# A fused attention and mixture-of-experts layer: maxima computed ten steps ahead instead of twelve, with weight loads, magnitudes and small steps placed at other ticks

## The reference, cut to what matters

```python
x = x + attn(layernorm(x))            # causal, softmax over keys
x = x + ffn(layernorm(x))

# attn
qkv = x @ W_qkv + b_qkv
scores = einsum('bhqd,bhkd->bhqk', q, k) * scale      # masked above the diagonal
out = (softmax(scores) @ v) @ W_out + b_out

# ffn: its own layernorm, a gate, then the two best of 8 experts
w, idx = top_k(softmax(xn @ gate_w), 2)
h = gelu(xn @ w1[e] + b1[e])
output = sum over the two of w * (h @ w2[e] + b2[e])  + residual
```

## Time and profile before

| | |
|---|---|
| median of 3 runs | 978.37 us (976.83 to 978.54) |
| the profiled execution, its own time | 980.76 us |
| its span | 979.0 us |
| mean granted TensorE clock | 0.902 |
| TensorE, VectorE, ScalarE, GpSimd busy | 89%, 74%, 60%, 47% |

### The profile page before, as it was taken

One profiled execution on the slowest core, in us unless ns is written; L12 is line 12 of the kernel. 1 busy time (PEld: TensorE's weight loads), 2 busy tenths in 40 slices (PEclk: granted clock), 3 DMA queues, 4 the chain that ended last, 5 costly groups with the idle time before them and its releaser, 6 DMA issues.

```text
span 979.0 us, 21326 instructions
## 1 busy us (share of the span) xinstructions
PE 867.6 (89%) x6870; PEld 564.8 (58%) x6870; DVE 724.6 (74%) x1658; ACT 586.0 (60%) x1079; POOL 462.0 (47%) x561
## 2 busy tenths in 40 slices
PE   4999977786876998888887899999999999999996
PEld 3655422231332424334342588889889989998874
DVE  6678886877657697898977488795776776666664
ACT  2776565554857687676958474564545554455453
POOL 2000032342525656558585656775476554545441
PEclk9999977775887758778897899999999999999999
DMA  9988667745747757566544742343323332233221
GB/s 211 298 278 255 203 183 206 188 119 161 215 133 211 198 153 210 139 204 168 168 123 126 237 105 60 61 92 54 51 40 57 52 57 48 46 50 48 44 45 17
DMA packets 146327, 130.09 MB, mean 133 GB/s; under 512 B 59344, under 2 KB 128848, under 8 KB 146096
## 3 DMA queue, kind: packets, MB, share of 16 engines
q1 hardware_dynamic: 115648, 87.51, 32.3%
q0 software_dynamic: 15680, 18.95, 12.1%
q10 hardware_dynamic: 14896, 22.28, 7.1%
HBM read 83.63 MB, written 44.80 MB: 131 GB/s over the span
## 4 chain that ended last, share of the span: by engine, by line
PE 45%; DMA 13%; DVE 12%; issue 10%; POOL 9%; SPq 6%; ACT 3%; POOLq 1%; ACTq 0%; DVEq 0%
PE banks L758 12%; PE banks L776 11%; PE banks L577 4%; POOL out L1693 3%; PE banks L680 3%; DMA weighed_values<-arena 3%; DMA arena<-qk_parts 3%; PE banks L636 3%; PE banks L567 2%; DMA arena<-in_L_ffn_w 2%; PE banks L692 2%; POOL slot_tokens L1640 2%; POOL arena L1669 2%; PE banks L608 2%; PE banks L621 2%
## 5 line engine op out<-in xcount | busy, mean ns | idle before, releaser
L980 ACT ACTIVATE arena<-banks,arena 128x256 f32<-128x256 f32 (+1 forms) x312 | 152.7, 542 | 175.7 <-issue 121.5
L758 PE MATMUL banks<-arena,weights 128*128 128x256 f16 (+1 forms) x1872 | 205.0, 266 | 4.5 <-DVE arena L1475 2.3
L776 PE MATMUL banks<-weights,arena 128*128 x1704 | 194.1, 273 | 0.6 <-DVE arena L1503 0.5
L758 PEld LDWEIGHTS banks<-arena,weights 128*128 x1872 | 174.4, 98 | 30.8 <-issue 7.3
L1693 POOL DMA_INDIRECT out<-arena x71 | 116.3, 1639 | 151.7 <-DVE arena L1514 114.3
L776 PEld LDWEIGHTS banks<-weights,arena 128*128 128x128 f16 x1704 | 165.6, 98 | 20.9 <-issue 1.8
L636 PE MATMUL banks<-arena 50*128 50x128 f16 (+3 forms) x512 | 129.2, 354 | 25.0 <-ACT arena L906 4.7
L608 PE MATMUL banks<-arena 48*128 48x128 f16 (+3 forms) x512 | 104.8, 352 | 44.0 <-DMA arena<-qk_parts 14.5
L1501 DVE TENSOR_SCALAR arena<-arena 128x512 f16<-128x512 f32 (+1 forms) x156 | 77.0, 493 | 62.9 <-ACT arena L980 61.5
L636 PEld LDWEIGHTS banks<-arena 50*128 50x128 f16 x512 | 38.9, 103 | 135.3 <-issue 55.0
L1503 DVE SCALAR_TENSOR_TENSOR arena<-arena 128x512 f16<-128x512 f32 (+1 forms) x156 | 110.1, 706 | 5.6
(11 more groups left out here) (190 smaller groups left out, 1309.3 us busy)
## 6 DMA issues: line engine op xcount, KB each, us to landing
weights<-in_L_ffn_w ACTq DMA_DIRECT2D x16, 1024.0 KB, 7.9
arena<-in_L_ffn_w SPq DMA_DIRECT2D x32, 512.0 KB
qk_parts<-weights SPq DMA_DIRECT2D x64, 128.0 KB
arena<-qk_parts SPq DMA_DIRECT2D x128, 64.0 KB, 3.2
weighed_values<-arena SPq DMA_DIRECT2D x32, 256.0 KB
token_rows<-arena SPq DMA_DIRECT2D x12, 512.0 KB, 4.4
arena<-qk_parts SPq DMA_DIRECT2D x128, 32.0 KB, 3.3
arena<-weighed_values SPq DMA_DIRECT2D x32, 128.0 KB
```

The costliest lines, as they stand in the source:

```text
L758: m = pe.matmul(bank[:, c * TILE:c * TILE + WIDTH[j]], w1[:, k, wp, f:f + P], xp[:, k, 0:WIDTH[j]], start=(i == 0), stop=(i == len(terms) ...
L776: m = pe.matmul(bank[:, c * D:(c + 1) * D], hp[:, f, c * P:(c + 1) * P], w2[:, f // (FC // 2), wp, f % (FC // 2), :], start=(f == 0 and i ...
L980: m = act.activation(h_32[r % 2][:, c, 0:WIDTH[j]], banks[:, 1 + c2, c * TILE:c * TILE + WIDTH[j]], ACT.Gelu, bias=b1_now[j % 2][:, 2 * c2 ...
```

## The change

`AHEAD` becomes 10: combo (u, i) computes slot i of unit u + 2, where it computed slot i + 2 of unit u + 2 (i up to 2) or slot i - 3 of unit u + 3. The projection computes ten slots instead of twelve, and starts them two steps of `project` later. The steps of the path of the maxima move with it. The last four magnitudes ahead of the attention (two matrices) are taken one by one in the first two units. The eight middle matrices are loaded in two halves each, 14 ticks apart. `invert`, `keep_inverse`, `move_inverse` and `divide` of the first eight units come 10 ticks later, `find_scales_2` 18 ticks later, and the first six weight splits 8 to 18 ticks later.

```diff
-        AHEAD = 2 * M_SLOTS + 2
+        AHEAD = 2 * M_SLOTS
...
-                at(base - 14, "top_split", u + 1)
-                at(base + 5, "top_turn", u + 1)
-                at(base + 10, "top_copy", u + 1)
-                at(base + 16, "top_in", u + 1)
+                at(base - 4, "top_split", u + 1)
+                at(base + 9, "top_turn", u + 1)
+                at(base + 14, "top_copy", u + 1)
+                at(base + 19, "top_in", u + 1)
...
-            at(after + (130 if late else 102), "invert", u)
-            at(after + (136 if late else 112), "keep_inverse", u)
-            at(after + (176 if late else 136 if u % NG else 158), "move_inverse", u)
+
+            room = 10 if u < 2 * NG else 0
+            at(after + (130 if late else 102 + room), "invert", u)
+            at(after + (136 if late else 112 + room), "keep_inverse", u)
+            at(after + (176 if late else 136 + room if u % NG else 158 + room), "move_inverse", u)
             if u % 2 == 1:
-                at(after + (216 if late else 156), "divide", divmod(u // 2, KC))
+                at(after + (216 if late else 156 + room), "divide", divmod(u // 2, KC))
         for i in range(len(matrices) - EARLY):
-            at(i * 36 + 30, "load_weights", i + EARLY)
-            at(i * 36 + 92, "magnitude", (i + EARLY, 0))
-            at(i * 36 + 110, "magnitude", (i + EARLY, 1))
+            at(i * 36 + 30, "load_weights", (i + EARLY, 0))
+            at(i * 36 + 44, "load_weights", (i + EARLY, 1))
+            at(i * 36 + 96, "magnitude", (i + EARLY, 0))
+            at(i * 36 + 114, "magnitude", (i + EARLY, 1))
+        for i in range(2):
+            for half in range(2):
+                at((8, 25, 44, 64)[2 * i + half], "magnitude", (EARLY - 2 + i, half))
...
-        at(8 * 36 + 114, "find_scales_2", 0)
-
-        split_ticks = [410 + 40 * i for i in range(LENT)]
+        at(8 * 36 + 132, "find_scales_2", 0)
+
+        split_ticks = [428 + 38 * i for i in range(LENT)]
...
-        OPEN = B - AHEAD // (2 * KC)
-        opening = [divmod(i, M_SLOTS) for i in range(AHEAD)]
+        OPEN = B + -AHEAD // (2 * KC)
+        opening = [None] * (2 * KC * (B - OPEN) - AHEAD) + [divmod(i, M_SLOTS) for i in range(AHEAD)]
...
-                    if b >= OPEN:
+                    if b >= OPEN and opening[2 * KC * (b - OPEN) + c]:
                         maxima(*opening[2 * KC * (b - OPEN) + c])
...
-            def load_weights(e_, m_):
+            def load_weights(e_, m_, halves=(0, 1)):
+                chunks = (KC, FC)[m_]
+                a, z = chunks * halves[0] // 2, chunks * (halves[-1] + 1) // 2
                 act.dma_start(
...
-                w.wait_ge(sem(f"w_in{m_}{e_}"), 16)
+                w.wait_ge(sem(f"w_in{m_}{e_}"), 16 if i < EARLY else 32)
...
-            magnitude(B - 2, (0, 1))
-            magnitude(B - 1, (0, 1))
             for stage, n in timetable:
```

More of the change, by code:

```diff
@@ L820, in load_x @@
                 act.dma_start(x_in[b % 4], x_rows(b)).then_inc(sem(f"x_in{b % 4}"), 16)
-            def load_weights(e_, m_):
+            def load_weights(e_, m_, halves=(0, 1)):
+                chunks = (KC, FC)[m_]
+                a, z = chunks * halves[0] // 2, chunks * (halves[-1] + 1) // 2
                 act.dma_start(
-                    w_sb[:, e_, m_ * EW // 2:(m_ + 1) * EW // 2].rearrange("p (c n) -> p c n", c=(KC, FC)[m_]),
-                    t[("L0_ffn_w1", "L0_ffn_w2")[m_]][e_].rearrange("(c p) n -> p c n", p=P)).then_inc(
+                    w_sb[:, e_, m_ * EW // 2:(m_ + 1) * EW // 2].rearrange("p (c n) -> p c n", c=chunks)[:, a:z, :],
+                    t[("L0_ffn_w1", "L0_ffn_w2")[m_]][e_].rearrange("(c p) n -> p c n", p=P)[:, a:z, :]).then_inc(
                     sem(f"w_in{m_}{e_}"), 16)
@@ L1038, in scalar @@
                         w.wait_ge(sem(f"v_store{half}"), 16 * (B // 2))
-                    load_weights(*matrices[n])
+                    load_weights(*matrices[n[0]], n[1:])
                 elif stage == "high_weights":
```

## The result

The changed kernel took 982.06 us (median of 7 runs, 981.06 to 988.52) beside 978.0 us for the kernel before: ratio 1.0053, interval 1.0031 to 1.0074. It is slower by 0.5%, where 1.6% faster was forecast, and lies outside the range. Run again in a later session it gave 1.0044 (1.0021 to 1.0068). The profiled execution took 984.82 us, its span is 983.0.

The account below looks back on a forecast made before the run. TensorE's waits in the attention, for stacks and VectorE, were taken as the bound. Projection -1, first ten units -14 and the others -1 sum to -16 us, giving 962.4 us; the range was 949 to 978.

Parts of the forecast that it names:

- Projection, -1: Before the attention: two slots fewer save 1.5 us, the transpose waits 0.5 for GpSimd's split; -1 us, bounds +1.2 and -2.2.
- First ten units, -14: Start of the attention: 124.1 us become 110, between VectorE's floor and the path of the maxima; bounds 105 and 118.
- the waits only move: Rival: VectorE stays at 78% in the first units and the removed waits return as others; 977 us, chance 0.07.
- The reciprocal comes 10 ticks later: First ten units: 2.6 us more room behind a sums' DMA that was 4.64 us late, so TensorE's 3.98 us wait goes.
- Queues: First units: changed order around `top_in`, GpSimd's split and masks, and TensorE's transpose costs nothing; uncovered, the third mask costs 1.2 us.
- `top_in` in the other units, "stays ahead": Behind the first eight units, on SyncE's queue: `top_in` still goes out before `keep_inverse`, so what it stands behind changes little.
- Halves, nothing: Middle matrices' loads: eight more issues, 3.1 us, hidden on ScalarE; the magnitude's lead of 14.1 us exceeds the longest landing.
- The scales later, a gain of the 2.51 and 5.04 us: First ten units: scales 18 ticks (4.7 us) later cover the 2.51 us DMA wait behind TensorE's 5.04 us wait.
- Magnitudes singly, -3.90: Attention's start: four magnitudes in a row take VectorE 4.59 us; taken singly, TensorE's 3.90 us wait goes.
- Units 10 to 31, -1: Rest of the attention: 5.5 us of stack waits and 1 of low clock go, split costs 4, two slots 1.5; bounds -7, +10.
- the clock comes back: Rival: the granted clock in units 10 to 31 rises from 0.81 to 0.9; 944 us, chance 0.15.
- the path of the maxima binds: Rival: through the attention, units pay the copy's 3.1 us delay; with seven such units 984 us, chance 0.11.

Follow-up runs that it names:

- e1: Kernel before with only the lead of the maxima cut to ten slots and its path (split, transpose, copy, `top_in`) moved: 1.0007 of the kernel before.
- e6: Changed kernel with `invert`, `keep_inverse`, `move_inverse` and `divide` of the first eight units back at their old ticks: 0.9968 of the kernel before.
- e10: Changed kernel with the sums' steps of the first eight units, `find_scales_2` and the first six weight splits at their old ticks: 0.9972 of the kernel before.
- e9: The changed kernel again as it is, in a later session as yardstick: 1.0044 of the kernel before.
- e14: Kernel before with only `invert`, `keep_inverse`, `move_inverse` and `divide` of the first eight units ten ticks later: 1.0060 of the kernel before.
- e15: Kernel before with only `invert` and `keep_inverse` of the first eight units ten ticks later: 1.0067 of the kernel before.
- e18: Kernel before with `invert` and `keep_inverse` ten ticks later, `move_inverse` and `divide` twenty, in the first eight units: 1.0002 of the kernel before.
- e11: Changed kernel with sums' steps, scales and splits at old ticks, and also the copy at tick 10 and `top_in` at 16: 0.9941 of the kernel before.
- e17: Kernel before with only the middle matrices loaded in halves, 14 ticks apart: 0.9966 of the kernel before.
- e8: Changed kernel with each middle matrix in one load of 1 MB in place of halves: 1.0110 of the kernel before.
- e7: Changed kernel with `find_scales_2` and the first six weight splits at their old ticks: 0.9991 of the kernel before.
- e13: Changed kernel with sums' steps, scales and splits at old ticks, and the four magnitudes again in a row ahead of the attention: 0.9967 of the kernel before.
- e12: Changed kernel with sums' steps, scales and splits at old ticks, and the old lead of twelve slots and old path: 0.9963 of the kernel before.

## Why the prediction was wrong

*The windows, and that TensorE after 552 passes everything on.* About right: the last scores of unit 31 come 5.7 us later (545.5 for 539.8), the profiled execution is 984.82 - 980.76 = 4.1 longer.

*Projection, -1.* Right: 120.7 to 119.0.

*First ten units, -14.* A size off: -6.3, at the bound that I had given (118 us). The waits named did go (stacks, three long VectorE waits). VectorE is busy 93.76 of 117.8 us, 80%, where 88% was forecast and 78% was the sign of "the waits only move". The path of the maxima was computed rightly (in unit 1 the copy ended 134.98 - 129.6 = 5.4 us after the unit's begin, 5.2 by the prediction) and costs little: with the new lead and path alone the ten units are 122.0 (e1). The landing of `top_in`, for which the sum took 5.0 and 3.5 us (the 3.5 with no row behind it), was 2.8 at most in unit 5. What kept them from 110 are single long holds, units 5 and 7 above all (16.0 and 15.6 us); with the ten ticks taken back they are 113.1 (e6), near the forecast, but only while the scales are late as well (119.0 in e10).

*"The reciprocal comes 10 ticks later", counted among the gains.* **This is the step that failed**, together with *Queues*, "these three cost nothing". Taken back, the ten ticks give 0.8% in the changed kernel, 7.4 us (e6 beside e9), and put alone on the kernel before they cost 0.6% (e14). The text weighed `keep_inverse` (tick 26 of a unit) against `top_in` (19) alone. It didn't see that `keep_inverse` also falls behind `move_o` (22), and `move_inverse` behind the next stack loads (44), though both of these can stand and wait on SyncE. In unit 5 `keep_inverse` so went out 4.8 us after its reciprocal and `top_in` 7.3 us after its copy, and in e6 0.7 and 1.3. That is shown for this unit. As a sum it is not: the first ten units carry 5.5 us of the 7.4 between e9 and e6, and SyncE's waits at `move_inverse` 2.5. On the kernel before, a hold of `move_inverse` is shown as the cause for e15, since with distance to `keep_inverse` the loss is gone (e18); e14, which has the changed kernel's own ticks, loses 0.6% without it. So which step failed is shown, and through which wait most of its price comes stays open.

*`top_in` in the other units, "stays ahead".* Ahead of `keep_inverse`, yes. But from tick 640 to 643 it passed a load of raw weights, which is 2.9 us of the one wait of 6.9 in unit 13; the prediction looked at one queued step only. Its old tick is the likely part of e11's 0.3%; the interval doesn't make it certain.

*Halves, nothing.* Wrong sign of a small term: -0.3% alone (e17), and 0.7% lost when they are taken out of the changed kernel (e8). I had looked at the lead of the magnitude and not at the small transfers that go between the halves. That these land sooner would be the natural reading, but the stack loads landed later with halves (3.8 and 4.0 us for 3.0 and 3.3, e17), so why the kernel gains stays open. The Trainium skill, "DMA: Bandwidth & Descriptors", section "Bandwidth", asks for transfers of at least 1 MiB for a high bandwidth. The trace agrees as to the loads themselves: 4.7 us for a half, 7.9 for a whole. For the kernel's time the rule decides nothing here: VectorE, which reads these matrices first, has no wait for them from 120 to 260 in either kernel.

*The scales later, a gain of the 2.51 and 5.04 us.* The wait went, and the first ten units gained by it (3.2 us between e7 and e9, 5.9 between e10 and e6). The price was the next term, "the later ticks of the splits [...] at no cost": the units behind lost 7.6 and 11.8 us. In unit 11 a split now stood 3.38 us on ScalarE for its raw weights, ahead of a copy that TensorE needed, and in unit 13 the stores of the splits held SyncE ahead of `top_in`. Together 0.5% was lost beside the sums' delay (e7), nothing without it (e10). *Magnitudes singly, -3.90.* The wait went and nothing came of it (e13): VectorE has the same work in those units wherever it stands.

*Units 10 to 31, -1.* +13.7 (295.0 to 308.7), of which unit 11 has 10.7 and the last twenty 1.8; +9.7 in the changed kernel's second profile (304.7). The split, 4 us in the forecast, is 13.2 over the whole attention. Unit 11 is the term that had no place in the sum: the prediction let the clock bring 1 us and allowed no loss, and this unit had run at the full clock in the kernel before, a place where it could only get worse. None of the other kernels' profiles has it at 1.00 again; it takes 14.5 us in e12, and 17.1 to 24.7 in the others. So a favourable unit 11 is probably part of the lead of the kernel before in its one profiled execution; the mean of 0.81 over all these units had hidden it from the prediction. In the first ten units the clock rose, from 0.75 to 0.83, and TensorE's work fell from 97.11 to 88.59 us; in the others it went from 0.81 to 0.79.

*The rivals.* In "the clock comes back", 256.1 us at 0.81 are 230 at 0.9 and not 229; nothing hangs on it. What came is nearest to "the path of the maxima binds". The sign set for it, over 20 us of waits for `top_in` and for GpSimd, was met with 17.9 + 13.2 = 31.1. But its mechanism, a copy 3.1 us later that every unit pays, is not what costs: e1 has it at 1.0007. `top_in` is late where SyncE's queue holds it, in a few units, and TensorE's two longest waits there are 4.6 and 6.9 us. The clause "it stands on SyncE's queue behind whatever that waits for" was the right one, and got no price.

## What to carry to other kernels

When a step moves, list for every queue it issues on what is now behind it, and ask for each of its waits when that is met; here two steps moved by ten ticks sent the next unit's data out 7.3 us late, though the wait of the one just ahead of it was only 2.6. A wait that disappears is a gain only where the engine that was late has less to do or more time; here 27 us of waits went and 45 came. Give a lasting wait of TensorE two prices: the wait, and the work that follows at the low clock, as in unit 11. Take each part of a bundled change back by itself in the same session: here one step lost 0.8% and hid that another, the halves, gains 0.3%.

## What the runs showed of the hardware

Sixteen loads of 512 KB landed in 4.7 us at the median, where 1 MB took 7.9 before and 8.4 in the same kernel; two halves so take longer in sum, and the kernel is faster with them.

One wait of TensorE cost more than itself. In unit 11 of the changed kernel the granted clock was 1.00 for the 4.7 us ahead of a wait of 3.94 us and 0.50 for the 13.3 us behind it. Some 110 matmul instructions kept TensorE busy 12.16 us at 1.00 in the kernel before, and 18.12 at 0.64 here; in the other kernels' profiles the unit's clock is 0.64 to 0.91.

A transfer of 8 KB can be slow to land. `keep_inverse` of unit 1 was issued by 170.54, and the step that waited for it went out at 178.26, with eight stack loads issued between.

The kernel before took 976.8 to 978.3 us in four of the sessions and 1002.8 and 1008.0 in two, 3% apart. The same chip gave 978.0, 1008.0 and 978.3 in three of them. The difference stands behind the attention: from the last scores of unit 31 to the end the profiled executions take 435 to 440 us in the one kind of session and 457 to 461 in the other. What makes it isn't shown.
